# Graph diffusion beside a dense stage: where a step's end rows come from, and when the next step's gathers are issued

## The reference, cut to what matters

```python
def _spmm(h, src, dst, inv_deg):
    msg = h[src]
    agg = jax.ops.segment_sum(msg, dst, num_segments=h.shape[0])
    return agg * inv_deg[:, None]

x = jax.nn.silu(h @ W_in.T + b_in)
term = out = x
for i in range(1, 7):
    term = _spmm(term, src, dst, inv_deg) / float(i)
    out = out + term
x = out @ W_out.T + b_out
```

## Time and profile before

| | us |
|---|---|
| median of 3 runs (lowest to highest) | 3920.31 (3916.71 to 3924.02) |
| span of the profiled execution | 3924.5 |
| busy: PE / DVE / POOL / ACT | 3261.1 / 2815.4 / 2087.1 / 1882.4 |
| first sum's add of the diffusion to its last bound sum's | 2417.5 to 3719.3 |

### The profile page before, as it was taken

One profiled execution on the slowest core, in us unless ns is written; L12 is line 12 of the kernel. 1 busy time (PEld: TensorE's weight loads), 2 busy tenths in 40 slices (PEclk: granted clock), 3 DMA queues, 4 the chain that ended last, 5 costly groups with the idle time before them and its releaser, 6 DMA issues. The chain is left out here.

```text
span 3924.5 us, 56642 instructions
## 1 busy us (share of the span) xinstructions
PE 3261.1 (83%) x14868; PEld 2626.7 (67%) x14868; DVE 2815.4 (72%) x7890; ACT 1882.4 (48%) x5403; POOL 2087.1 (53%) x2120
## 2 busy tenths in 40 slices
PE   5999927688576899477999993599999999999865
PEld 4888715476454566245777772587878787888754
DVE  5676768698587466794666662598989898989733
ACT  3777705466333121142333331366666666666555
POOL 4767500475365666033333322476767676767667
PEclk8999958899799999657999996799999999999998
DMA  5788739443375333183333335886868686878765
GB/s 145 244 244 247 235 95 354 153 134 108 107 211 174 94 88 87 54 247 99 111 116 115 111 110 187 283 252 199 251 201 252 197 251 201 253 208 242 209 210 164
DMA packets 690467, 710.71 MB, mean 181 GB/s; under 512 B 73444, under 2 KB 644190, under 8 KB 689796
## 3 DMA queue, kind: packets, MB, share of 16 engines
q1 hardware_dynamic: 592204, 484.13, 39.8%
q0 software_dynamic: 68288, 181.26, 17.1%
q10 hardware_dynamic: 29660, 41.70, 3.2%
HBM read 427.77 MB, written 296.22 MB: 184 GB/s over the span
## 5 line engine op out<-in xcount | busy, mean ns | idle before, releaser
L616 POOL DMA_INDIRECT s_i_messages<-h,table_row x600 | 614.0, 1023 | 190.4 <-issue 158.3
L2801 PE MATMUL s_i_bank<-s_i_messages,s_i_equal 128*128 128x256 f32 x1200 | 362.5, 386 | 74.3 <-issue 36.6
L926 POOL TENSOR_TENSOR n_powers<-n_powers,neg_half 128x8 f32<-128x8 f32 (+3 forms) x164 | 268.5, 1637 | 229.9 <-DVE n_powers L891 149.4
L851 ACT ACTIVATE n_z<-gamma_bc,n_powers 128x256 f32<-128x256 f32 x320 | 174.8, 593 | 356.5 <-POOL n_powers L926 356.5
L810 PE MATMUL s_n_bank<-w,n_xt 128*128 128x256 f32 x1280 | 306.9, 383 | 22.6 <-DMA n_xt<-in_x_t 22.6
L828 PE MATMUL s_n_bank<-w_out,n_ht 128*128 128x256 f32 x1280 | 311.7, 387 | 5.6 <-ACT n_ht L838 5.3
L2838 DVE SCALAR_TENSOR_TENSOR s_i_y<-s_i_bank,s_i_scale,s_i_acc 128x256 f32<-128x256 f32 x600 | 285.2, 476 | 34.3 <-PE s_i_bank L2801 32.2
L819 PE MATMUL s_n_bank<-n_x3t,w_in 128*128 128x256 f32 x1280 | 303.2, 380 | 0.0
L2801 PEld LDWEIGHTS s_i_bank<-s_i_messages,s_i_equal 128*128 128x128 f32 x1200 | 219.3, 193 | 101.1 <-issue 42.2
L810 PEld LDWEIGHTS s_n_bank<-w,n_xt 128*128 128x128 f32 x1280 | 246.0, 192 | 58.0 <-DMA n_xt<-in_x_t 23.8
L828 PEld LDWEIGHTS s_n_bank<-w_out,n_ht 128*128 128x128 f32 x1280 | 247.3, 195 | 46.2 <-ACT n_ht L838 11.9
(11 more groups left out here) (444 smaller groups left out, 9169.7 us busy)
## 6 DMA issues: line engine op xcount, KB each, us to landing
h<-s_i_y SPq DMA_DIRECT2D x600, 128.0 KB, 3.9
n_xt<-in_x_t SPq DMA_DIRECT2D x160, 256.0 KB
out<-n_w SPq DMA_DIRECT2D x160, 256.0 KB
s_i_equal<-eq_tab SPq DMA_DIRECT2D x600, 64.0 KB
x<-s_x_rows SPq DMA_DIRECT2D x100, 256.0 KB
out<-s_a_hs SPq DMA_DIRECT2D x100, 128.0 KB
proj_dst<-s_a_hd SPq DMA_DIRECT2D x100, 128.0 KB
h<-s_h_rows SPq DMA_DIRECT2D x50, 256.0 KB, 4.1
```

The source lines that it names most:

```text
L616: return net.nc.gpsimd.indirect_dma_start(out, None, table, bass.IndirectOffsetOnAxis(index, 0))
L851: sc = self.nc.scalar.activation(self.Z[u][:, g, :], self.net.bc["gamma"][:], ACT.Identity, bias=v[:, 8 + g:9 + g], scale=v[:, 10 + g:11 + g])
L926: self.nc.gpsimd.tensor_tensor(v[:, 8 + b0:8 + b1], v[:, b0:b1], self.net.neg_half[:, 0:b1 - b0], ALU.pow).then_inc(self.powered, 1)
L2801: nc.tensor.matmul(banks[r % 4][:, 0:D], EQ[q % NM][:], M[q % NM][:], start=True, stop=True).then_inc(summed, 1)
```

## The change

The bound sum moves from place 105 of its step to 103. Each store is issued one place behind the sum and not two, and with it goes a second, small copy, from the first two rows of `Y` in SBUF to the tile's partition of `EF`; the load from DRAM and its semaphore are gone. Both copies count on the buffer's semaphore, so the waits for it ask for 32 and not 16, and PE's bound sum waits for all ten of these semaphores itself. The gathers of the next step may start at place 107 (three behind POOL's place for the scatter), where they started at 106, and from place 8 of the program on at most one goes out at a place.

```diff
--- before.py
+++ after.py
@@ -2679,7 +2679,7 @@
         g0, g1 = gaps * s // STEPS, gaps * (s + 1) // STEPS
         for t in range(T):
             at[g0 + t * (g1 - g0 - 9) // T] = (s, t)
-        at[g1 - 5] = (s, T)
+        at[g1 - 7] = (s, T)
     assert len(at) == STEPS * (T + 1)
     return at
 
@@ -2705,8 +2705,8 @@
         B = st.sb("i_bound", [T, D])
         scale = st.sb("i_scale", [P, STEPS, T])
         acc_in, got, eq_in, stored = st.sem("i_acc_loaded", T // CHUNK), st.sem("i_gathered", NM), st.sem("i_eq_loaded", NM), st.sem("i_stored", NY)
-        scale_ready, summed, added, ends_in, scattered, copied = (
-            st.sem(f"i_{n}") for n in ("scale_ready", "summed", "added", "ends_loaded", "scattered", "copied"))
+        scale_ready, summed, added, scattered, copied = (
+            st.sem(f"i_{n}") for n in ("scale_ready", "summed", "added", "scattered", "copied"))
         assert T % NM == 0 and T % NY == 0 and T % CHUNK == 0
         TURNS = dn.units + 5
         GAPS = TURNS * dn.PIECES
@@ -2729,19 +2729,15 @@
                 q = s * T + t
                 sp.wait_ge(added, nth(s, t))
                 sp.dma_start(tabs[(s + 1) % 2][t * P:(t + 1) * P, :], Y[q % NY][:]).then_inc(stored[q % NY], 16)
-
-            def load_ends(s):
-                for b in range(NY):
-                    sp.wait_ge(stored[b], 16 * (T // NY) * (s + 1))
-                sp.dma_start(EF[:], tabs[(s + 1) % 2][0:R, :].rearrange("(t p) d -> t p d", p=P)[:, 0:2, :]).then_inc(ends_in, 16)
+                sp.dma_start(EF[t:t + 1, :, :], Y[q % NY][0:2, :]).then_inc(stored[q % NY], 16)
+
+
             n = itertools.count()
 
             def gap():
                 i = next(n)
-                if i - 2 in at and at[i - 2][1] < T:
-                    store(*at[i - 2])
-                    if at[i - 2][1] == T - 1:
-                        load_ends(at[i - 2][0])
+                if i - 1 in at and at[i - 1][1] < T:
+                    store(*at[i - 1])
                 if i in at and at[i][1] < T:
                     load_eq(at[i][0] * T + at[i][1] + AHEAD)
             for u in range(2):
@@ -2777,8 +2773,11 @@
                     s, t = at[i - 1]
                     if t == T:
                         put_bound(s)
-                    upto_q = min((s + 1) * T if t < T else STEPS * T, s * T + t + AHEAD + 1)
-                for k in range(2):
+                    else:
+                        upto_q = min((s + 1) * T, s * T + t + AHEAD + 1)
+                if i - 4 in at and at[i - 4][1] == T and at[i - 4][0] + 1 < STEPS:
+                    upto_q = (at[i - 4][0] + 1) * T + AHEAD
+                for k in range(2 if i < AHEAD else 1):
                     if fetched < upto_q:
                         get(fetched)
                         fetched += 1
@@ -2793,7 +2792,8 @@
                 if r >= 4:
                     pe.wait_ge(added, r - 3)
                 if t == T:
-                    pe.wait_ge(ends_in, 16 * (s + 1))
+                    for b in range(NY):
+                        pe.wait_ge(stored[b], 32 * (T // NY) * (s + 1))
                     nc.tensor.matmul(banks[r % 4][0:T, 0:D], net.upper[:], EF[:, 0, :], start=True, stop=True).then_inc(summed, 1)
                 else:
                     pe.wait_ge(eq_in[q % NM], 16 * (q // NM + 1))
@@ -2834,7 +2834,7 @@
                     if s == 0 and t % CHUNK == 0:
                         dve.wait_ge(acc_in[t // CHUNK], 16)
                     if q >= NY:
-                        dve.wait_ge(stored[q % NY], 16 * (q // NY))
+                        dve.wait_ge(stored[q % NY], 32 * (q // NY))
                     V.scalar_tensor_tensor(Y[q % NY][:], banks[r % 4][:, 0:D], scale[:, s, t:t + 1], acc[:, t, :], ALU.mult, ALU.add).then_inc(added, 1)
             n = itertools.count()
 
```

## The result

The changed kernel takes 3969.76 us (3968.46 to 3972.55, four runs) against 3919.91 for the kernel before beside it: a ratio of 1.0128, 95% interval 1.0114 to 1.0142, 49.9 us slower. The forecast was 3957 in 3900 to 4010. The profiled execution has a span of 3966.7 us.

A forecast was written before the change was run, and what follows sets the result against it. PE was taken to bound the long steady stretches, with a hole at each of five step changes. Gain of 34 us there and 71 us lost to late gathers sum to +37: 3957 us, range 3900 to 4010.

The forecast's parts named there:

- The lead: Gathers on POOL: each turn's first would start only 2.67 us before its sum and land late, losing 71 us.
- 12.02 + L: Length of the two-turn loop through PE, ACT, DVE, POOL and the gather; each turn grows by (L - 2.67) / 2.
- L: Landing time of a turn's first gather, taken as 3.8 us, between 2.8 and 4.6.
- the first rival: The gathers land in time, so only the 34 us gain is left: 3886 us; chance 0.16.
- The hole: Lost time at each of five step changes, 8.8 us a step, to shrink to 2: gain 34 us.
- The 2.5 us that PE was to wait at the bound: PE's predicted wait at the earlier bound sum, for the last copy's landing in place of the load.
- The end rows: Small copies on SP, 0.30 to 0.47 us each: its burst of 6.4 to 7.0 us still fits the 7.345 turn.
- the third rival: SP becomes the bound: copies at 0.6 us with gap, a burst of 7.36 us, result 4021; chance 0.06.
- L = 3.4 with the large: Gather landing of 3.4 us paired with the large hole gain, given as one way to the forecast's lower end, 3930.
- the 44 of the range: Upper bound of the gain at the step changes: 8.8 us per step over five steps.
- What was to be seen: Signs if right: PE waits for gathers in most turns, powers each 7.9 us, steps about 216 us apart.
- The sign against it: SP without idle time between bursts would show the forecast wrong and the third rival right.

The follow-up runs named there:

- experiment 2: Kernel before with only the new gathers' rule (one a place, from three places ahead of the sum), no small copies: 3952.5 us.
- experiment 8: Changed kernel with its small copies issued by ACT instead of SP, gathers still three places ahead of their sum: 3948.2 us.
- experiment 7: Changed kernel with gathers starting one place sooner, four ahead of their sum, and all 600 small copies issued by ACT instead of SP: 3887.7 us.
- experiment 10: Changed kernel with small copies issued by ACT and the old gathers' rule, two a place right behind the scatter: 3925.6 us.
- 6: Kernel before, end rows from DRAM and bound sum at 105, with gathers paced anew four places ahead of their sum: 3900.9 us.
- experiment 3: Changed kernel with gathers starting one place sooner, four places ahead of their sum, small copies still on SP: 3924.9 us.
- experiment 5: Changed kernel with gathers four places ahead; only each step's last ten tiles copied, the other ninety loaded from DRAM in one piece: 3898.6 us.

## Why the prediction was right, and where it was not

**The lead: right in mechanism, and in size per turn.** Predicted was a loop of two turns, 12.02 + L, with L = 3.8: a turn of 7.91, 0.565 us longer, 71 us. Experiments 2 and 8, without copies on SP, have turns of 7.91 and 7.93, and 8 less 7 is 0.57 a turn. The whole cost is less: 60.5 us between the medians of 8 and 7, where 71 was written. The two windows leave out the turns next to a bound; over all sums of steps 1 to 5 four of them take 7.88 us in experiment 8 and 7.34 in 7, 0.54 more, or 67 us, and the hole of 8 is smaller than that of 7 by 0.8 us a step. L was also chosen rightly: the median of all gathers is 3.8. The choice went by the second gather of a burst as the nearest row, and the first stall shown above has 3.92. The Trainium skill's "DMA: Bandwidth & Descriptors", section Anatomy of one DMA — SWDGE (gpsimd) path, by which they would have landed in time (an estimate of 2.3 us), did not hold for this load; the measurement decides. So the first rival, gathers in time, needs one place more of lead. Then it is right: 3887.7 in experiment 7, where 3886 was written, though only with SP relieved as well.

**The hole: size right, place wrong.** Predicted were 34 us. By the table's rest they are 37, over all sums 33, and the seventh experiment, which has no loss in its turns, gains 33. They were put down to the bound sum's move, with only the 2.90 us of POOL's wait for the scatter to the gathers' new place. But the changed hole is there without that move (1.6 in experiment 2), and the move without the pacing gains nothing (10.1 in experiment 10). What empties the hole is that the powers no longer stand behind the wait for the scatter and a row of gathers on POOL. The move adds 13 us, with the end rows, once the gathers are paced with lead four (6 to 7); with lead three it is 4 (2 to 8). The 2.5 us that PE was to wait at the bound are 3.3 at the first and 15.7 over six, as long as before.

**The end rows: the step that failed.** "6.4 to 7.0 of 7.345 still fits: nothing on the path." The copy was priced between the load's 0.30 and a store's 0.47 us, and has 0.57, or 0.62 with its gap; the burst is 7.26 us, and in experiment 3 the same list takes 7.23 to 7.35 even without a long issue: no room is left in 7.345, and it came onto the path. The argument against the third rival, that a load of 100 end rows took SP 0.30 us, was no bound, for the number of bytes or rows is not what sets this time. The rival's threshold, 0.6 us with the gap, was met; its consequence was not. Landings did not go to 4.6 (3.8) and the kernel not to 4021. With lead three the turn is 7.93 without any copy on SP (experiment 8), so SP still has some room beside the gathers' stall: from 2920 to 3070 us it waits for a result 8.6 us in ten places. SP costs 0.11 us a turn, 14 us by the turns and 21.6 by the medians, on top of the lead (3.5 of the rest lies in step 0, which takes 257.7 us to its bound sum's add and 254.2 in experiment 8), and 37.2 us where the lead is long enough (3 less 7). The two costs overlap; they don't add.

By the experiments one after the other, from before to 7, to 8 and to the change, the sum is -33 + 60.5 + 21.6 = +49, measured +49.9. Predicted was -34 + 71 + 0 = +37. So the 13 us by which the forecast was short are the copies, 22, less the 10 by which the lead was put too high; that these two go against each other is luck.

One bound of the forecast is put together unevenly: "L = 3.4 with the large" gain gives 3930 only with the middle gain of 34; with the 44 of the range it would be 3922.

**What was to be seen.** PE waits for gathers 84 times in 125 turns, 0.7 us in the mean (predicted: most turns, about 1 us), and the waits from 2680 us on already hold all 84: none is in step 0. Powers every 8.04 us (7.9), steps 218.6 apart (216), DVE's 7.61 us gone, and POOL's wait for the scatter down to two places. The sign against it, SP without idle time between bursts, is nearly there: its waits from 2920 to 3070 us add up to 14.9, where the kernel before has 61.1. That sign should have been given its own price inside the forecast and not only at 4021.

## What to carry to other kernels

A transfer that is issued one step closer to its use belongs in a loop with the engine that waits for it: sum up the loop, put the landing measured under load in it, and divide by the turns that it spans. Here that gave the steady turn to the hundredth of a microsecond and the whole loss to 10 us in 60, and one place more of lead takes it away. Behind a barrier, short work that others wait for should go ahead of a burst of prefetches. Count the issue time of small DMAs on the queue that issues them, by their number and not their bytes, and if they fill it, issue them where another engine waits anyway, but look first for the buffer that comes free only with the store that is moved.

## What the hardware showed that was not expected

A copy of two rows of 1 KB from SBUF to one partition of SBUF holds its issuing queue for 0.57 us, on SP (570/571 ns, 600 times) as on ACT (565/566), while a 200 KB load of two rows for each of 100 partitions takes 0.30 and a 128 KB store 0.47. When that load is cut to 90 partitions it takes 0.35 (experiment 5), and beside it the small copies have 0.57 again:

```profile
L2733 SPq DMA_DIRECT2D s_i_ends<-s_i_y x60: 570/570/677, 2635.2 to 3678.5; - x60
...
L2741 SPq DMA_DIRECT2D s_i_ends<-h x6: 344/350/520, 2646.1 to 3673.8; - x6
```

Of these the smallest transfer is the dearest to issue. The Trainium skill has something that would fit, in "DMA: Bandwidth & Descriptors", section Why a DMA increments its semaphore by 16 and not by 1: a transfer that runs on fewer than 16 DMA engines has the issuing queue make up the missing counts itself. No run here varied the number of partitions of the small copy, so whether that is where the time goes isn't shown.

Also, the median landing of gathers fell from 4.4 to 3.8 us (3.8 in experiment 2 as well) when they were spread out and the DMA share went from 0.86 to 0.79: whether in bursts they had waited for each other or for the rest of the traffic was not parted; the lead of seven places hid it.
